# Grouped-query attention: value products in three fp32r products, two units behind the scores; rope sums and output parts on GpSimd

## The chip, the cores and the metric

One core of a Trainium2 chip runs the whole program in one launch. The metric is the device time of that launch in microseconds (us). The kernel before takes 2538.56 us, the median of three runs (2532.92 to 2539.3). Within 0.3% two kernels can't be told apart here.

## The reference

Two layers work on 1024 tokens (two batches of 512) of width 512. Each layer is attention and a feed-forward part, and after each of the four the result is added to its input and normalised. The change touches only the attention of the second layer, grouped-query attention with 32 query heads and 8 key/value heads of width 128:

```python
q = (hidden_states @ Wq).reshape(B, S, nh, hd).transpose(0, 2, 1, 3)
k = (hidden_states @ Wk).reshape(B, S, nkv, hd).transpose(0, 2, 1, 3)
v = (hidden_states @ Wv).reshape(B, S, nkv, hd).transpose(0, 2, 1, 3)
q = _apply_rope(q, cos, sin)        # x * cos + rotate_half(x) * sin
k = _apply_rope(k, cos, sin)
...                                 # k, v repeated for the 4 heads of a group
logits = jnp.einsum('bhqd,bhkd->bhqk', q, k) * scale      # then the causal mask
attn = jax.nn.softmax(logits.astype(jnp.float32), axis=-1).astype(q.dtype)
out = jnp.einsum('bhqk,bhkd->bhqd', attn, v)
return out.transpose(0, 2, 1, 3).reshape(B, S, nh * hd) @ Wo
```

## The kernel before

The stages run one after the other. In the stage of the change (`gqa_stage`) five engines run programs of their own, each in the order in which it is written, and wait for each other by counting semaphores. Each program is a loop over the eight key heads (`body`). The last body stands apart, since it has no next head to prepare.

A body has eight units (`NU`), one for each pair of a query head of the group (four) and a batch half (two). Unit `u` belongs to head `u // 2` and batch `u % 2`. Nearly every product is made in three: a number is split into a high part (rounded to fp32r) and a low part (the rest), and high x high, low x high and high x low are added up in PSUM (`TERMS`). Making the parts is a copy and a subtraction.

For a unit, TensorE first makes the scores of four row tiles (L1570 to L1583). A row tile `t` has (t + 1) * 128 columns, for the causal mask; together they take three banks (`ps_s`). VectorE takes the row maxima (L1484), ScalarE the exponentials with their row sums (L1423), VectorE the reciprocals (L1489) and the scaling of the rows in place (`normalise`, four instructions at L1493, SBUF to SBUF). TensorE transposes the rows in three pieces of 4, 4 and 2 tiles into two banks `ps_t` (L1593), pieces 1 and 3 of a unit in the same bank; ScalarE copies each piece to SBUF (L1430). TensorE multiplies it with the values in fp32 (`outputs`, L1603); this product alone is not made in three. ScalarE takes the high part of the result (L1436) and VectorE the low part (L1499).

The query of a unit is projected by 12 matmuls (L1558) two units ahead. Its rope is on VectorE: two multiplications by the sine into `by_sin` with the halves swapped (L1473, L1474), one by the cosine into `roped` (L1475), and the sum (L1477). GpSimd then makes the high part (L1357) and the low part (L1359) of the sum. GpSimd also splits the weights of this and the next head (L1337, L1339), one slice (two instructions) behind each rope. SP's queue loads the next weights once the old ones are split.

In a unit's turn `u`, TensorE's order is: scores of `u`, pieces 1 and 2 of `u - 1`, projection of the query of `u + 2`, piece 3 of `u - 1`, outputs of `u - 1`. VectorE's order is: maxima of `u`, normalise of `u`, rope of `u + 2`, low part of the outputs of `u - 1`. In turns 6 and 7 the next body's keys and queries are projected, in place of a query of this one (two projections and two ropes in each turn). After the eight turns each body multiplies the outputs of its four heads by their rows of `Wo` (`merge`, eight token tiles of 12 matmuls, L1614), and VectorE adds the result to `X` (L1520). At the start of a body, between the scores of unit 0 and unit 1, the values are projected, copied (L1410), transposed (L1567) and copied to `v1` (L1414).

## Time and profile before

| | us |
|---|---|
| median of three runs | 2538.56 |
| the profiled execution | 2530.54 |
| its span | 2528.8 |
| attention of the second layer, 1640 to 2465 | 825 |

| engine, whole span | busy us |
|---|---|
| TensorE, matmul | 2460.4 |
| TensorE, weight load | 1857.2 |
| VectorE | 1557.3 |
| ScalarE | 1393.4 |
| GpSimd | 1136.3 |

In the rows below PE is TensorE's matmul, PEld its weight load, DVE VectorE, ACT ScalarE and POOL GpSimd. L1593 is line 1593 of the kernel before. The durations of matmuls run into each other, since they are pipelined: what one costs is the distance from its start to the next start, its pitch.

### The profile page before, as it was taken

The page shows a single profiled execution, that of the slowest core. Times are in us where ns is not written, and L with a number is a line of the kernel's source. Part 1 is how long each engine was busy: PE and PEld are TensorE (multiplying, and loading weights), DVE is VectorE, ACT ScalarE, POOL GpSimd, SP SyncE. Part 2 cuts the span into 40 slices and gives each one's busy share as a digit, 9 for nine tenths or more (in the row PEclk, how much of TensorE's full clock was granted, in tenths as well). Part 3 has the DMA queues.
Part 4 walks back from the last instruction along what each step waited for, and adds up shares of the span by engine and source line. Part 5 has one row for each costly group of instructions (what it writes and reads, how often), then busy time and mean ns, then how long its engine had stood idle before and what let it go on. Part 6 is the DMA issues. An engine that isn't in the chain of part 4 may idle for free. (4 is left out here: it accounts for less than half of the span.)

```text
span 2528.8 us, 40532 instructions
## 1 busy us (share of the span) xinstructions
PE 2460.4 (97%) x12630; PEld 1857.2 (73%) x12630; DVE 1557.3 (62%) x2790; ACT 1393.4 (55%) x2155; POOL 1136.3 (45%) x1140
## 2 busy tenths in 40 slices
PE   8999999999999999999998999899999999999997
PEld 4777777777777777777775688687787887878774
DVE  7666666666666666666664523474755756557556
ACT  4777777777777777777776423242423424324231
POOL 1555555565656555555554334143424335234210
PEclk9999999999999999999999999999999999999998
DMA  6222222222222222222223222101001000010001
GB/s 214 45 53 44 53 47 58 45 53 44 53 47 53 45 53 53 44 53 44 55 49 88 96 88 88 71 26 42 17 25 41 16 26 18 23 41 17 1 1 55
DMA packets 47611, 125.39 MB, mean 50 GB/s; under 512 B 6033, under 2 KB 23441, under 8 KB 41426
## 3 DMA queue, kind: packets, MB, share of 16 engines
q1 hardware_dynamic: 47570, 124.85, 18.4%
q8 instruction: 25, 0.41, 0.1%
q14 instruction: 16, 0.13, 0.0%
HBM read 80.27 MB, written 10.49 MB: 36 GB/s over the span
## 5 line engine op out<-in xcount | busy, mean ns | idle before, releaser
L427 DVE TENSOR_REDUCE row_max<-ps_max 128x1 f32<-128x512 f32 x1024 | 670.8, 688 | 187.6 <-PE ps_max L517 165.5
L292 POOL TENSOR_TENSOR p_parts<-probs,p_parts 128x1024 f16<-128x1024 f32 x256 | 547.6, 2149 | 360.1 <-ACT p_parts L346 359.1
L341 ACT ACTIVATE probs<-ps_score 128x1024 f32<-128x1024 f32 x512 | 523.4, 1023 | 238.9 <-PE ps_score L533 217.0
L531 PE MATMUL ps_score<-Q,K 128*128 128x512 f32 x1024 | 406.9, 397 | 2.7 <-ACT probs L341 2.2
L533 PE MATMUL ps_score<-Q,K 97*128 97x512 f32 x1024 | 406.3, 397 | 0.0
L517 PE MATMUL ps_max<-KX,Q 68*128 68x512 f32 x1024 | 377.9, 410 | 2.4 <-DVE row_max L427 2.3
L421 DVE TENSOR_TENSOR Q<-ps_x,Q 64x512 fp32r<-64x512 f32 x254 | 175.1, 689 | 241.1 <-ACT Q L336 237.4
L346 ACT ACTIVATE p_parts<-probs 128x1024 f16<-128x1024 f32 x256 | 269.5, 1053 | 4.1
L517 PEld LDWEIGHTS ps_max<-KX,Q 68*128 68x128 f32 x1024 | 189.1, 189 | 74.4 <-issue 27.3
L531 PEld LDWEIGHTS ps_score<-Q,K 128*128 128x128 f32 x1024 | 194.0, 189 | 60.7 <-ACT probs L341 9.6
L1357 POOL CAST q_hi<-roped 128x512 fp32r<-128x512 f32 x64 | 39.2, 612 | 416.5 <-DVE roped L1477 198.4
L533 PEld LDWEIGHTS ps_score<-Q,K 97*128 97x128 f32 x1024 | 194.7, 190 | 39.7
L1423 ACT ACTIVATE probs<-ps_s,minus_max 128x512 f32<-128x512 f32 (+3 forms) x256 | 131.8, 541 | 138.5 <-DVE minus_max L1484 138.5
L1430 ACT ACTIVATE probsT<-ps_t 128x512 f32<-128x512 f32 (+1 forms) x192 | 94.1, 525 | 176.2 <-PE ps_t L1593 175.8
L336 ACT ACTIVATE Q<-ps_x 64x512 fp32r<-64x512 f32 x254 | 150.7, 593 | 72.5 <-PE ps_x L502 71.0
L1603 PE MATMUL ps_o<-probsT,v 128*128 128x512 f32 (+3 forms) x512 | 149.2, 434 | 1.3 <-ACT probsT L1430 1.3
L502 PE MATMUL ps_x<-xl,w_hi 128*128 128x512 f32 x508 | 143.6, 405 | 0.0
L502 PE MATMUL ps_x<-xh,w_hi 128*128 128x512 f32 x508 | 139.2, 396 | 0.0
L502 PE MATMUL ps_x<-xh,w_lo 128*128 128x512 f32 x508 | 138.4, 395 | 0.0
L1436 ACT ACTIVATE o_hi<-ps_o 128x512 fp32r<-128x512 f32 x64 | 38.4, 599 | 168.0 <-PE ps_o L1603 168.0
L544 PE MATMUL ps_o<-probs,V_slot 128*32 128x512 f32 x1024 | 123.1, 598 | 3.4 <-ACT probs L341 3.4
L1520 DVE TENSOR_TENSOR X<-ps_r,X 128x512 f32<-128x512 f32 x64 | 44.3, 692 | 132.9 <-PE ps_r L1614 132.9
(269 smaller groups left out, 4418.6 us busy)
## 6 DMA issues: line engine op xcount, KB each, us to landing
Q<-Q SPq DMA_DIRECT2D x64, 512.0 KB, 4.3
ffn_raw<-in_w_ffn SPq DMA_DIRECT2D x22, 768.0 KB, 4.3
w_raw<-in_w_qrope SPq DMA_DIRECT2D x32, 512.0 KB, 3.6
wq_raw<-in_wq SPq DMA_DIRECT2D x8, 1024.0 KB, 5.5
wo_raw<-in_wo SPq DMA_DIRECT2D x8, 1024.0 KB, 4.9
content_k<-probs SPq DMA_DIRECT2D x8, 512.0 KB, 6.4
Q<-content_q SPq DMA_DIRECT2D x64, 64.0 KB
K<-content_k SPq DMA_DIRECT2D x64, 64.0 KB
```

The source lines that it names most:

```text
L292: pool.tensor_tensor(p_lo[:, j, :, :], probs[:, j, 0:PAIRED, :], p_hi[:, j, :, :], ALU.subtract)\
L336: ins = act.activation(Q2[0:ROPE, b, 2 * pair + k, :], src[k * ROPE:(k + 1) * ROPE, :], ACT.Copy)
L341: act.activation(probs[:, j, 2 * half:2 * half + 2, :], ps_score[half][:, :, :], ACT.Exp, scale=SCALE).then_inc(exped, 1)
L346: act.activation(p_hi[:, j, :, :], probs[:, j, 0:PAIRED, :], ACT.Copy).then_inc(p_high, 1)
L421: ins = dve.tensor_tensor(Q1[ROPE:P, b, 2 * pair + k, :], src[k * ROPE:(k + 1) * ROPE, :], Q2[0:ROPE, b, 2 * pair + k, :], ALU.subtract)
L427: dve.tensor_reduce(row_max[:, t, j:j + 1], ps_max[t % 2][:, :], axis=AXX, op=ALU.max)\
L502: last = pe.matmul(out[:, :], w[:, c, pair, :], sb[x][:, c, b * S:(b + 1) * S], start=third == c == 0, stop=third == 2 and c == DC - 1)
L517: pe.matmul(ps_max[t % 2][:, :], Q2[0:KC0, b, j, t * P:(t + 1) * P], KX[0:KC0, b, j, :], start=True, stop=True).then_inc(max_made, 1)
L531: pe.matmul(ps_score[half][:, k, :], K1[:, b, t * P:(t + 1) * P], Q1[:, b, j, :], start=True, stop=False)
L533: last = pe.matmul(ps_score[half][:, k, :], K2[0:MROW + 1, b, j, t * P:(t + 1) * P], Q2[0:MROW + 1, b, j, :], start=False, stop=True)
L1423: act.activation(probs[:, u % 2, t, 0:n], ps_s[bank][:, at:at + n], ACT.Exp, bias=minus_max[:, t:t + 1], accum_out=sums[:, u % 2, t:t + 1] ...
L1603: last = pe.matmul(ps_o[:, tile * P:S], V[:, b, tile, :], probsT[:, k, at:at + S - tile * P], start=tile == 0, stop=k == 2)
```

## The change

- Value products are made in three, as the others: `V` and `probsT` get a high and a low part. ScalarE copies the high parts; VectorE makes the low parts, of the values (`low_values`) and of the three pieces of each unit (`low_turned`). A bank `ps_t` is free once the low part is made. `outputs` has 12 matmuls where it had 4 in fp32.
- The outputs of a unit and piece 3 of its transposes go one turn later: TensorE's order in turn `u` is scores of `u`, piece 3 of `u - 2`, projection, outputs of `u - 2`, pieces 1 and 2 of `u - 1`.
- VectorE's order in turn `u` is: maxima of `u`, low part of piece 3 of `u - 2`, rope of `u + 2` without its sum, normalise of `u`, low parts of pieces 1 and 2 of `u - 1`.
- The rope's sum moves to GpSimd, in front of its high and low part. `by_sin` has two buffers.
- ScalarE copies the outputs unsplit to `o_raw` (two buffers), and GpSimd makes both parts (`split_out`), behind the rope of the unit four later.
- The rows of a unit are packed in `probs` one behind the other (1280 numbers) in place of four rows of 512.
- The merges begin with the heads that are ready: they go head by head, with waits for the last two. Piece 3 of unit 7 and its outputs stand between the merges.

```diff
-        V = buf("v1", [P, NB, ST, P])
-        by_sin = buf("by_sin", [P, S])
+        V = [buf(f"v_{k}", [P, NB, ST, P], F32R) for k in ("hi", "lo")]
+        by_sin = buf("by_sin", [P, 2, S])
         roped = buf("roped", [P, 2, S])
-        probs = buf("probs1", [P, 2, ST, S])
-        probsT = buf("probsT", [P, 3, S])
+        ROWS = [P * t * (t + 1) // 2 for t in range(ST + 1)]
+        probs = buf("probs1", [P, 2, ROWS[ST]])
+        TURNED = [(0, S), (S, S), (2 * S, 2 * P)]
+        probsT = [buf(f"probsT_{k}", [P, 2 * S + 2 * P], F32R) for k in ("hi", "lo")]
+        values_T = probs[:, 1, 0:NB * S].rearrange("p (b s) -> p b s", b=NB)
+        o_raw = buf("o_raw", [P, 2, S])
...
-            def rope(n, at, parts):
-
+            def rope(n, at, parts, take):
+
+                pool.wait_ge(taken, take + 1)
+                pool.sem_inc(gate_pool, 1)
+                pool.tensor_tensor(roped[:, at, :], roped[:, at, :], by_sin[:, at, :], ALU.add).then_inc(summed, 1)
                 pool.wait_ge(summed, n + 1)
                 pool.sem_inc(gate_pool, 1)
                 pool.tensor_copy(parts[0], roped[:, at, :]).then_inc(r_high, 1)
                 pool.wait_ge(r_high, n + 1)
+                pool.sem_inc(gate_pool, 1)
                 pool.tensor_tensor(parts[1], roped[:, at, :], parts[0], ALU.subtract).then_inc(r_low, 1)
...
+            def split_out(i, u):
+
+                pool.wait_ge(o_taken, ONE + i + 1)
+                pool.sem_inc(gate_pool, 1)
+                pool.tensor_copy(O[0][:, u % 2, u // 2, :], o_raw[:, u % 2, :]).then_inc(o_step, 1)
+                pool.wait_ge(o_step, i + 1)
+                pool.sem_inc(gate_pool, 1)
+                pool.tensor_tensor(O[1][:, u % 2, u // 2, :], o_raw[:, u % 2, :], O[0][:, u % 2, u // 2, :],
+                                   ALU.subtract).then_inc(o_low, 1)
...
-                    rope_query(r + u - 2, u, u % 2)
+                    rope_query(r + u - 2, u, u % 2, tk + take_query(u))
+                    if u >= 4:
+                        split_out(i + u - 4, u - 4)
...
-                        rope_key(r + NU - 2 + 2 * b, b)
-                        rope_query(r + NU - 1 + 2 * b, b, 1)
+                        rope_key(r + NU - 2 + 2 * b, b, tk + take_next(2 * b))
+                        if b == 1:
+                            split_out(i + NU - 3, NU - 3)
+                            split_out(i + NU - 2, NU - 2)
+                        rope_query(r + NU - 1 + 2 * b, b, 1, tk + take_next(2 * b + 1))
                         if b == 0:
+                            split_out(i + NU - 4, NU - 4)
                             split_kv(1, s + n + 1)
+                    split_out(i + NU - 1, NU - 1)
                     for h in range(1, GQ):
                         split_q(h, s + n + 1 + h)
+                else:
+                    for u in range(NU - 4, NU):
+                        split_out(i + u, u)
 
...
+                act.wait_ge(o_low, i + 1)
+                act.activation(o_raw[:, u % 2, :], ps_o[:, :], ACT.Copy).then_inc(o_taken, 1)
...
+                softmax(i, 0, ALL)
                 values(kv, 0)
                 values(kv, 1)
                 turned_values(kv, 0)
                 turned_values(kv, 1)
                 for u in range(1, NU):
+                    if u >= 2:
+                        act.wait_ge(turned, 3 * (i + u - 1))
+                    softmax(i + u, u, BEGIN)
+                    if u >= 2:
+                        take_turned(kv, u - 2, 2)
+                    softmax(i + u, u, REST)
+                    if u >= 2:
+                        take_outputs(kv, u - 2)
                     take_turned(kv, u - 1, 0)
                     take_turned(kv, u - 1, 1)
-                    softmax(i + u, u)
-                    take_turned(kv, u - 1, 2)
-                    take_outputs(kv, u - 1)
+                take_turned(kv, NU - 2, 2)
+                take_outputs(kv, NU - 2)
...
-                dve.tensor_tensor(by_sin[0:h, :], ps[h:P, :], tables[0:h, sin, :], ALU.mult)
-                dve.tensor_tensor(by_sin[h:P, :], ps[0:h, :], tables[h:P, sin, :], ALU.mult)
+                dve.tensor_tensor(by_sin[0:h, at, :], ps[h:P, :], tables[0:h, sin, :], ALU.mult)
+                dve.tensor_tensor(by_sin[h:P, at, :], ps[0:h, :], tables[h:P, sin, :], ALU.mult)
                 dve.tensor_tensor(roped[:, at, :], ps[:, :], cos, ALU.mult).then_inc(taken, 1)
-                dve.wait_ge(taken, take + 1)
-                dve.tensor_tensor(roped[:, at, :], roped[:, at, :], by_sin[:, :], ALU.add).then_inc(summed, 1)
...
+            def low_values(kv, b):
+                dve.wait_ge(v_high, NB * kv + b + 1)
+                dve.tensor_tensor(V[1][:, b, :, :], ps_t[b][:, :].rearrange("p (t n) -> p t n", t=ST), V[0][:, b, :, :],
+                                  ALU.subtract).then_inc(v_low, 1)
+
+            def low_turned(i, u, k):
+                dve.wait_ge(t_high, 3 * i + k + 1)
+                at, n = TURNED[k]
+                dve.tensor_tensor(probsT[1][:, at:at + n], ps_t[(u + k) % 2][:, 0:n], probsT[0][:, at:at + n],
+                                  ALU.subtract).then_inc(t_low, 1)
...
+                for b in range(NB):
+                    low_values(kv, b)
                 rope(r, ring + ring_query(2), (START + ring_query(2)) % 2, 0, tk, 0)
+
+                def rope_next(at):
+                    rope(r + NU - 2 + at, ring + ring_next(at), (START + ring_next(at)) % 2, 1 - at % 2,
+                         tk + take_next(at), at % 2)
+
                 for u in range(1, NU):
                     maxima(i + u)
-                    normalise(i + u, u)
+                    if u >= 2:
+                        low_turned(i + u - 2, u - 2, 2)
                     if u < NU - 2:
                         rope(r + u, ring + ring_query(u + 2), (START + ring_query(u + 2)) % 2, 0, tk + u, u % 2)
-                        low_o(i + u - 1, u - 1)
-                    else:
-                        for k in range(2) if not last else ():
-                            at = 2 * (u % 2) + k
-                            rope(r + NU - 2 + at, ring + ring_next(at), (START + ring_next(at)) % 2, 1 - k, tk + take_next(at), k)
-                        low_o(i + u - 1, u - 1)
+                    elif not last:
+                        for at in (0, 1) if u == NU - 2 else (2,):
+                            rope_next(at)
+                    normalise(i + u, u)
+                    low_turned(i + u - 1, u - 1, 0)
+                    low_turned(i + u - 1, u - 1, 1)
+                low_turned(i + NU - 2, NU - 2, 2)
+                if not last:
+                    rope_next(3)
+                low_turned(i + NU - 1, NU - 1, 0)
+                low_turned(i + NU - 1, NU - 1, 1)
                 add_out(0)
-                add_out(1)
-                low_o(i + NU - 1, NU - 1)
-                for j in range(2, TT):
+                low_turned(i + NU - 1, NU - 1, 2)
+                for j in range(1, TT):
...
-                pe.wait_ge(o_low, ONE + i)
-                for k, piece in enumerate(pieces):
-                    pe.wait_ge(t_taken, 3 * i + k + 1)
-                    for tile, at in piece:
-                        last = pe.matmul(ps_o[:, tile * P:S], V[:, b, tile, :], probsT[:, k, at:at + S - tile * P],
-                                         start=tile == 0, stop=k == 2)
+                pe.wait_ge(o_taken, ONE + i)
+                for p, vs in ((0, (0, 1)), (1, (0,))):
+                    for k, piece in enumerate(pieces):
+                        pe.wait_ge((t_high, t_low)[p], (0, TWO)[p] + 3 * i + k + 1)
+                        for v in vs:
+                            for tile, at in piece:
+                                at += TURNED[k][0]
+                                last = pe.matmul(ps_o[:, tile * P:S], V[v][:, b, tile, :],
+                                                 probsT[p][:, at:at + S - tile * P],
+                                                 start=tile == p == v == 0, stop=k == 2 and p == 1)
                 last.then_inc(pv_made, 1)
...
-            def merge(last, tk, j):
+            def merge(last, tk, i, j):
 
                 at = ring_out(last, j)
                 pe.wait_ge(taken, tk + take_out(last, j) - 1)
                 k = 0
-                for o, w in TERMS:
-                    for h in range(GQ):
+                for h in range(GQ):
+                    if j % ST == 0 and h >= GQ - 2:
+                        pe.wait_ge(o_low, TWO + i + 2 * h + j // ST + 1)
+                    for o, w in TERMS:
...
                     scores(i + u, u, r + u - 2)
-                    if u == 1:
-                        pe.wait_ge(v_ready, NB * (kv + 1))
-                    turn(i + u - 1, u - 1, 0)
-                    turn(i + u - 1, u - 1, 1)
+                    if u >= 2:
+                        turn(i + u - 2, u - 2, 2)
                     if u < NU - 2:
                         query(u + 2)
                     elif not last:
-                        b = u % 2
-                        pe.wait_ge(wkv_split, 2 * kv + 3)
-                        pe.wait_ge(taken, tk + take_next(2 * b) - 1)
-                        project(wkv, 0, b, (START + ring_next(2 * b)) % 2)
-                        pe.wait_ge(wq_split, GQ * (kv + 1) + 1)
-                        pe.wait_ge(taken, tk + take_next(2 * b + 1) - 1)
-                        project(wq, 0, b, (START + ring_next(2 * b + 1)) % 2)
-                    turn(i + u - 1, u - 1, 2)
-                    outputs(i + u - 1, u - 1)
-                for k in range(3):
-                    turn(i + NU - 1, NU - 1, k)
+                        key_next(u % 2)
+                        if u == NU - 2:
+                            query_next(0)
+                    if u >= 2:
+                        outputs(i + u - 2, u - 2)
+                    if u == 1:
+                        pe.wait_ge(v_low, NB * (kv + 1))
+                    turn(i + u - 1, u - 1, 0)
+                    turn(i + u - 1, u - 1, 1)
+                turn(i + NU - 2, NU - 2, 2)
+                if not last:
+                    query_next(1)
+                outputs(i + NU - 2, NU - 2)
+                turn(i + NU - 1, NU - 1, 0)
+                turn(i + NU - 1, NU - 1, 1)
                 pe.wait_ge(wo_split, GQ * (kv + 1))
-                pe.wait_ge(o_low, ONE + i + NU - 1)
-                merge(last, tk, 0)
-                merge(last, tk, 1)
+                merge(last, tk, i, 0)
+                turn(i + NU - 1, NU - 1, 2)
+                merge(last, tk, i, 1)
+                merge(last, tk, i, 2)
                 outputs(i + NU - 1, NU - 1)
-                merge(last, tk, 2)
-                merge(last, tk, 3)
-                pe.wait_ge(o_low, ONE + i + NU)
-                for j in range(ST, TT):
-                    merge(last, tk, j)
+                for j in range(3, TT):
```

## Rows read from the trace of the kernel before

**Rows 1.** Windows: window, its length, busy time and instructions of each engine, clock granted, DMA.
```profile
1640.00:2465.00 825.00, 809.46 (x4156) 662.20 (x4154) 508.92 (x1032) 288.08 (x806) 292.83 (x312) 1.00 0.06 22
```

**Rows 2.** Waits of TensorE, 1640 to 2465: who for whom, total, times, longest.
```profile
PE ps_r L1614 <- DVE o_lo L1499: 9.0, 7, 1.3
```

**Rows 3.** Timeline of TensorE, one turn: start, duration, engine, line, operation.
```profile
1904.17 1.06 PE L1593 MATMUL ps_t<-ident,probs 128*128 128x128 f32 x8
1904.98 1.18 PE L1558 MATMUL ps_r<-xh,wq_hi 128*128 128x512 f32 x4
...
1908.05 2.32 PE L1603 MATMUL ps_o<-probsT,v 128*128 128x512 f32 x8
1910.02 0.58 PE L1580 MATMUL ps_s<-k_hi,q_hi 128*128 128x512 f32 x1
1910.44 0.40 PE L1580 MATMUL ps_s<-k_hi,q_lo 128*128 128x512 f32 x1
1910.67 0.39 PE L1580 MATMUL ps_s<-k_lo,q_hi 128*128 128x512 f32 x1
...
1911.37 0.34 PE L1580 MATMUL ps_s<-k_lo,q_hi 128*128 128x384 f32 x1
1911.55 0.22 PE L1581 MATMUL ps_s<-mask_sb 128*128 128x128 f32 x1
1911.61 0.27 PE L1580 MATMUL ps_s<-k_hi,q_hi 128*128 128x128 f32 x1
...
1912.52 1.05 PE L1593 MATMUL ps_t<-ident,probs 128*128 128x128 f32 x8
```

**Rows 4.** Timeline of the same turn, VectorE and GpSimd.
```profile
1901.16 0.69 DVE L1473 TENSOR_TENSOR by_sin<-ps_r,tables 64x512 f32<-64x512 f32 x1
...
1903.29 0.69 DVE L1477 TENSOR_TENSOR roped<-roped,by_sin 128x512 f32<-128x512 f32 x1
...
1903.90 0.68 DVE L1499 TENSOR_TENSOR o_lo<-ps_o,o_hi 128x512 fp32r<-128x512 f32 x1
...
1904.14 0.61 POOL L1357 CAST q_hi<-roped 128x512 fp32r<-128x512 f32 x1 [4.43 <-DVE roped L1477]
...
1904.50 1.68 DVE L1484 TENSOR_REDUCE minus_max<-ps_s 128x1 f32<-128x512 f32 x4
...
1907.98 0.18 DVE L1489 RECIPROCAL inverse<-sums 128x4 f32<-128x4 f32 x1 [1.80 <-ACT probs L1423]
...
1908.19 1.28 DVE L1493 TENSOR_SCALAR probs<-probs,inverse 128x128 f32<-128x128 f32 x4
```

**Rows 5.** First body's normalise beside GpSimd, then L1493 from 1662 on (ns min/median/max).
```profile
1656.56 1.30 POOL L1339 TENSOR_TENSOR wq_lo<-wq_raw,wq_hi 128x512 fp32r<-128x512 f32 x1
1656.80 3.61 DVE L1493 TENSOR_SCALAR probs<-probs,inverse 128x128 f32<-128x128 f32 x4
1657.80 0.61 POOL L1337 CAST wq_hi<-wq_raw 128x512 fp32r<-128x512 f32 x1
1658.49 1.29 POOL L1339 TENSOR_TENSOR wq_lo<-wq_raw,wq_hi 128x512 fp32r<-128x512 f32 x1
...
L1493 DVE TENSOR_SCALAR probs<-probs,inverse x252: 285/382/489, 1668.1 to 2436.9; 128x128 f32<-128x128 f32 x63, 128x384 f32<-128x384 f32 x63
```

**Rows 6.** Timeline at the start of a body, all engines.
```profile
1967.38 1.07 PE L1558 MATMUL ps_r<-xh,wq_hi 128*128 128x512 f32 x4
...
1970.51 0.69 DVE L1473 TENSOR_TENSOR by_sin<-ps_r,tables 64x512 f32<-64x512 f32 x1 [4.09 <-PE ps_r L1558]
...
1970.77 1.09 ACT L1414 ACTIVATE v<-ps_t 128x512 f32<-128x512 f32 x2 [2.59 <-PE ps_t L1567]
1970.92 0.48 PE L1580 MATMUL ps_s<-k_hi,q_hi 128*128 128x512 f32 x1
```

**Rows 7.** Timeline of TensorE: the first score matmul of two bodies in a row.
```profile
1857.03 0.39 PE L1580 MATMUL ps_s<-k_hi,q_hi 128*128 128x512 f32 x1
...
1959.54 0.39 PE L1580 MATMUL ps_s<-k_hi,q_hi 128*128 128x512 f32 x1
```

More of the change, by code:

```diff
@@ L1358, in rope, with rope_key, rope_query @@
                 pool.wait_ge(r_high, n + 1)
+                pool.sem_inc(gate_pool, 1)
                 pool.tensor_tensor(parts[1], roped[:, at, :], parts[0], ALU.subtract).then_inc(r_low, 1)
-            def rope_key(n, b):
-                rope(n, 0, [k[:, b, :] for k in K])
-            def rope_query(n, u, at):
-                rope(n, at, [q[:, u % 2, :] for q in Q])
+            def rope_key(n, b, take):
+                rope(n, 0, [k[:, b, :] for k in K], take)
+            def rope_query(n, u, at, take):
+                rope(n, at, [q[:, u % 2, :] for q in Q], take)
+            def split_out(i, u):
[6 more added lines that the diff above has]
+                                   ALU.subtract).then_inc(o_low, 1)
+            pool.sem_inc(o_low, TWO)
             for b in range(NB):
-                rope_key(2 * b, b)
-                rope_query(2 * b + 1, b, 1)
+                rope_key(2 * b, b, 2 * b)
+                rope_query(2 * b + 1, b, 1, 2 * b + 1)
             pool.wait_ge(wq_split, 2)
@@ L1376, in body @@
                 s = FIRST + GQ - 2 + EACH * kv
+                tk = START + TAKEN * kv
+                i = NU * kv
                 n = 0
@@ L1409, in values, with softmax @@
                 act.wait_ge(made, START + PER * kv + b + 1)
-                act.activation(probsT[:, b, :], ps_r[(START + b) % 2][:, :], ACT.Copy).then_inc(v_taken, 1)
+                act.activation(values_T[:, b, :], ps_r[(START + b) % 2][:, :], ACT.Copy).then_inc(v_taken, 1)
             def turned_values(kv, b):
                 act.wait_ge(v_turned, NB * kv + b + 1)
-                act.activation(V[:, b, :, :], ps_t[b][:, :].rearrange("p (t n) -> p t n", t=ST), ACT.Copy)\
-                   .then_inc(v_ready, 1)
-            def softmax(i, u):
-                for k, t in enumerate((3, 2, 0, 1)):
+                act.activation(V[0][:, b, :, :], ps_t[b][:, :].rearrange("p (t n) -> p t n", t=ST), ACT.Copy)\
+                   .then_inc(v_high, 1)
+            def softmax(i, u, part):
+                for k, t in list(enumerate((3, 2, 0, 1)))[part]:
                     act.wait_ge(maxed, ST * i + (3 if k == 1 else k + 1))
@@ L1422, in softmax @@
                     n = (t + 1) * P
-                    act.activation(probs[:, u % 2, t, 0:n], ps_s[bank][:, at:at + n], ACT.Exp,
+                    act.activation(probs[:, u % 2, ROWS[t]:ROWS[t] + n], ps_s[bank][:, at:at + n], ACT.Exp,
                                    bias=minus_max[:, t:t + 1], accum_out=sums[:, u % 2, t:t + 1]).then_inc(exped, 1)
@@ L1465, in rope @@
                 dve.wait_ge(made, ring + 1)
-                if not first:
-                    dve.wait_ge(summed, n)
                 if not first and not second:
@@ L1566, in turn_values @@
                 for t in range(ST):
-                    last = pe.transpose(ps_t[b][:, t * P:(t + 1) * P], probsT[:, b, t * P:(t + 1) * P], ident[:, :])
+                    last = pe.transpose(ps_t[b][:, t * P:(t + 1) * P], values_T[:, b, t * P:(t + 1) * P], ident[:, :])
                 last.then_inc(v_turned, 1)
```

43 lines of the change are left out of this document (25 added, 18 removed).

## The prediction, made before the changed kernel ran

> **What bounds the kernel now.** I read the windows first: the changed stage is 825 of 2528.8 us and TensorE is busy in 809.5 of them, VectorE in 509, ScalarE in 288 and GpSimd in 293, with TensorE's clock granted in full (the 2.4 GHz level) [rows 1]. The waits of TensorE in it are small; the largest is 1.3 us, once for each key head but the last [rows 2]. So before the change TensorE's order of work is the length of the stage. The timeline of one inner unit (one head of one batch half; 64 of them, eight in each of eight bodies) repeats every 8.35 us (1904.17 to 1912.52) [rows 3]. What decides this prediction are VectorE and GpSimd, which have room in the sum, and the question whether they have it at the same moments.
>
> **Value products (TensorE).** The fp32 products of a unit are eight records from 1908.05 to 1910.02, and the first score matmul behind them takes 0.42 to the next (1910.44), where an fp32r matmul of 512 columns has a pitch of 0.23 (1910.44 to 1910.67): 1.97 and 0.19 of change-over, 2.16 us [rows 3]. New are three products of four matmuls: 512 columns at 0.23, 384 at 0.18 (1911.37 to 1911.55), 128 at 0.06 behind a long one (1911.55 to 1911.61), 256 between these two, I take 0.12, and some 0.05 lost behind each short one: 1.9 us. Bounds: 1.77 (nothing lost behind the short ones) and 2.1 (each 128 and 256 a tenth dearer than I take them). Scores now follow fp32 transposes; what that change-over costs I bound by 0 and the 0.19 just read, and take 0.1. Gain: 0.16 us for a unit, 1.3 for a body, 10 in all, if TensorE remains the bound (-0.1 to 0.39 a unit, -6 to 25 in all).
>
> **Other work moved.** VectorE loses the rope sum (0.69, 80 times) and the low part of the outputs (pitch 0.60, 64 times) and gains three low parts of the transposed rows per unit (0.60, 0.60 and some 0.35, by the 0.60 pitch and half the columns): about +0.3 us a unit [rows 4]. Two low parts of the values are added per body (0.69 each). ScalarE does the same number of copies, in another order; it is 35% busy, so this costs nothing unless it delays what it feeds. GpSimd gains a rope sum, which it never ran here: bounds 0.61 (its cast, one input) and 2.6 (twice its subtraction), and I take the subtraction's own 1.30, which has the same shape and two inputs [rows 5]; what it is longer or shorter goes straight into the loop below. It gains an output split too (0.69 + 1.24 by start-to-start [rows 5]). Its step is then 1.37 + 0.69 + 1.24 for the rope, 1.93 for the outputs and 1.93 for a weight split: 7.2 us in a unit of 8.2. It fits, and the weight loads behind it on SP's queue move some 13 us later in a body, where they have over 30 us. Packed rows and the second by_sin buffer change addresses only: no term.
>
> **Where the wait appears.** In the new order VectorE runs: maxima, low part 3 of the unit before last, three rope multiplications, normalise, low parts 1 and 2. TensorE's transposes of piece 3 (in front of the next query projection) wait for low part 1, because they write the same bank; the projection feeds the rope; the rope stands in front of the normalise on VectorE; and that in front of low part 1. This is a loop, with length
> 0.2 (release, by the 0.16 from VectorE's end at 1903.98 to GpSimd's start at 1904.14 [rows 4]) + 0.2 (two transposes at 0.10, eight in 0.81 [rows 3]) + 0.1 + 3.13 (projection's first matmul to the rope's first instruction, 1967.38 to 1970.51 [rows 6]) + 2.13 (three multiplications, 1901.16 to 1903.29 [rows 4]) + N + 0.69 (low part 1) = 6.45 + N.
> N runs from the rope's last multiplication to the end of the normalise. In before it is 1.5 (reciprocal at 1907.98, its scalings to 1909.47 [rows 4]). Then the loop is 7.95 us and hides under TensorE's 8.2.
>
> **What N becomes.** Four scalings take 1.28 us together in rows 4, where GpSimd is idle. One of the 64 normalises met a busy GpSimd: its four took 3.61 us (1656.80 to 1660.41) while GpSimd ran 1656.56 to 1657.86, 1657.80 to 1658.41 and 1658.49 to 1659.78 at its usual durations; the other 252 scalings were never above 489 ns [rows 5]. Three scalings, each behind one whole GpSimd instruction, explain it: the fourth, with GpSimd done, was quick. VectorE instructions that read PSUM show nothing of this: the maxima at 1904.50 take their 1.68 beside GpSimd's split from 1904.14 [rows 4]. In before the normalise stands ahead of the rope and GpSimd idles 4.4 us until the rope is summed [rows 4]. The change puts it right behind the rope's last multiplication, and this is also what starts GpSimd's sum: 0.17 later, the first scaling 0.24 later. So each scaling meets one of: sum, cast, subtraction, and the cast of the next split. The fourth ends 0.17 + 1.37 + 0.69 + 1.24 + 0.61 + 0.37 = 4.45 after the rope, or 4.1 if it slips in ahead of the next cast; I take N = 4.3. Bounds: 1.5 (as before) and 4.45. The loop is 10.75 us against 8.2, and TensorE stands still for the rest: its cheaper products lie inside this wait and return nothing.
>
> A rule of the Trainium skill speaks against this change: "SBUF — State Buffer", section "SBUF: two separate sides", says that VectorE in a mode with two ports and GpSimd exclude each other for a whole instruction rather than share. With that rule, the trace agrees in the one place it can (3.61 against 1.28). Were bandwidth shared instead, N would be nearer 2.8, which is the second rival.
>
> **The sum for a body**, from its first score matmul. The values' second copy ends at 1971.86 and scores of unit 1 start 11.38 after the body's [rows 6]; behind it low parts of values to 13.1, rope of unit 2 to 15.3, GpSimd's sum, cast and subtraction to 18.8. Scores of unit 2 would be due at 17.4 (11.38 + 2.38 + 2.75 + 0.9): they wait 1.6 us. Maxima of unit 1 to 16.9, rope of unit 3 to 19.05, normalise with GpSimd busy (weights, then its sum) to 23, first piece-3 transposes at 23.9. Then four loops of 10.75 (66.9), one of 10.75 + 2.75 with the next key projection (80.4), one of 10.75 (91.2), last query projection, outputs, eight transposes (5.9, to 97.1), and eight merges of 12 x 0.228 with one piece 3 and one outputs (24.0): 121.1 us. Before it is 102.5 (1857.03 to 1959.54 [rows 7]). Seven bodies: 7 x 18.6 = 130. The last has no next projections; units 1 to 5 lose 2.5 + 4 x 2.4, and some 1.5 where nothing fills a wait: 14. Start of the stage: scores of unit 0 wait for GpSimd's two longer ropes, 1. Together +145 us on the profiled execution's 2530.5 (span 2528.8 and 1.7 around it): 2676. The median of the runs shown is 8 us above that execution; I forecast 2680 between both.
>
> **Rivals.**
> 1. *The scalings are not held up* (N stays under 1.7). For it: one single case in before carries the argument; against it: three scalings in a row were stretched there, and the collision is triggered by the same event in each unit. Then per body: -1.3 products, +1.6 at the start, +0.4 at the end (piece 3 of unit 6 waits 2.0 in place of 0.3 + 1.3), +0.7 in all, with 1 and 2 at the ends of the stage +8: 2546 by the median.
> 2. *Half held up*: only one or two scalings wait, N near 2.8, loop 9.25; seven loops less 1.5 in eight bodies is 80 less: 2600.
> 3. *Faster*: as 1, and the three products cost their 1.77 with no change-over, 0.39 a unit or 3.1 a body, against 2.0 lost at start and end: -1.1 a body, 2530. It decides from N under 1.7 and more than 0.25 us gained per unit; against it that fp32r matmuls of 128 columns show a pitch that their columns don't explain.
> 4. *GpSimd late with the output parts*: merge 0 needs unit 6's, 2.8 us after its products; it has 2.9. If late by one split, +1.9 a body: 2695, inside my range.
>
> **Chances.** Forecast with 4: 0.72 (2640 to 2720). Rival 2: 0.09. Rival 1: 0.10, most of it within the 0.3% (7.6 us) that a measurement of this kernel can't tell from no change. Rival 3: 0.09. Slower 0.72 + 0.09 + 0.03 = 0.84, same 0.07, faster 0.09. Range 2575 to 2725: it takes in N from 2.8 up and leaves out rivals 1 and 3.
>
> **What would show it.** Scalings of the normalise with means of 0.9 us and more where they were 0.30 to 0.48, the stage near 970 us, TensorE's largest wait on VectorE's low part of the transposed rows some 2.5 us per unit, and busy shares of TensorE in the stage falling from 98% to near 83%. Product group at 1.9 us by start-to-start. Wrong if the scalings keep their 0.30 to 0.48 with GpSimd busy, or if scores, not piece 3, are what waits.

## The result and the profile after

The changed kernel takes 2613.57 us (median of 4 runs, 2607.76 to 2617.49) against 2538.93 (4 runs, 2532.92 to 2542.43): slower by the ratio 1.0294, interval 1.0272 to 1.0315. The forecast was 2680 with a range of 2575 to 2725. The sign came as forecast, and scalings held up by GpSimd are the cause, as forecast; the size is about half. The band of 2640 to 2720, which had 0.72, is missed. The time lies in the range only because the range reaches down to rival 2 (2600), which had 0.09.

The windows of the changed stage, of one body with the clock granted in full and of the last body. The columns are those of [rows 1]: length, then busy time and instructions of PE, PEld, DVE, ACT and POOL, the granted clock, the DMA share and GB/s.

```profile
1640.00:2546.00 906.00, 823.62 (x4444) 707.46 (x4442) 620.57 (x1113) 291.00 (x819) 528.13 (x524) 0.98 0.06 23
2109.00:2218.95 109.95, 100.50 (x554) 86.72 (x552) 75.54 (x136) 35.70 (x101) 66.76 (x66) 1.00 0.07 23
2443.60:2546.00 102.40, 91.63 (x505) 78.64 (x503) 72.06 (x133) 34.19 (x100) 43.04 (x42) 0.98 0.00 1
```

Against [rows 1] this window is 81 us longer, and TensorE is busy in 91% of it where it was 98%. Of the 81 us, 11 lie ahead of the stage: its first projection starts at 1648.73, in before at 1637.57. A body at the full clock takes 109.95 us where it took 102.5 [rows 7]. VectorE is busy 112 us more (620.6 against 508.9). Some 20 of them are work: the low parts that it gained are 119 us (81.7 + 27.2 + 10.3), the rope sums and output parts that it lost 99 (55.4 + 43.8). Another 88 are the scalings, which are as many as before and are held up. By form, the four scalings of the normalise in the stage (busy time, mean ns of one | idle ahead):

```profile
L1534 DVE TENSOR_SCALAR probs<-probs,inverse 128x256 f32<-128x256 f32 x64 | 70.4, 1100 | 0.0
L1534 DVE TENSOR_SCALAR probs<-probs,inverse 128x512 f32<-128x512 f32 x64 | 56.2, 879 | 0.0
L1534 DVE TENSOR_SCALAR probs<-probs,inverse 128x384 f32<-128x384 f32 x64 | 35.9, 560 | 0.0
L1534 DVE TENSOR_SCALAR probs<-probs,inverse 128x128 f32<-128x128 f32 x64 | 25.9, 404 | 2.2
```

In before these forms took 354, 482, 433 and 300 ns, 100.5 us together; now it is 188.4. The 256 columns take three times their time, the 512 not quite twice; the 384 and the 128 take some 0.1 us more. These means mix units of different kinds, which are told apart below. The waits of the stage (us in total, times, longest):

```profile
POOL roped L1364 <- DVE roped L1517: 212.0, 51, 20.2
PE ps_t L1650 <- DVE probsT_lo L1545: 61.8, 56, 2.8
PE ps_s L1638 <- POOL q_lo L1370: 13.3, 9, 1.5
```

TensorE's large wait is the one forecast, the transposes of piece 3 for VectorE's low part 1, 56 times, but at 1.1 us a time, not 2.5 (0.57 in the units of the loop). The first row says that GpSimd's sum waits for the end of VectorE's rope, 51 times for 80 sums, so the two are in step in most units. Two groups of GpSimd show a thing that the sum had left out (stage up to 2460; the last figure is the idle time ahead):

```profile
L1346 POOL TENSOR_TENSOR wq_lo<-wq_raw,wq_hi 128x512 fp32r<-128x512 f32 x30 | 38.8, 1294 | 2.4
L1370 POOL TENSOR_TENSOR q_lo<-roped,q_hi 128x512 fp32r<-128x512 f32 x58 | 74.1, 1278 | 10.4 <-POOL q_hi L1367 10.4
```

Both subtractions wait for the cast ahead of them. The first, which the change leaves alone, starts 0.08 us (2.4 / 30) behind it. The second, where the change puts one more signal (`pool.sem_inc(gate_pool, 1)`) between the two, starts 0.18 us (10.4 / 58) behind. The same signal stands between the sum and the cast of the rope. So the change, besides moving work to GpSimd, opens gaps of 0.17 to 0.18 us in it.

One unit in the timeline (start, duration, engine; in brackets the idle ahead and what ended it). VectorE, with the four scalings one by one:

```profile
1931.73 0.69 DVE L1517 TENSOR_TENSOR roped<-ps_r,tables 128x512 f32<-128x512 f32 x1
1932.55 0.29 DVE L1534 TENSOR_SCALAR probs<-probs,inverse 128x128 f32<-128x128 f32 x1
1932.75 1.38 DVE L1534 TENSOR_SCALAR probs<-probs,inverse 128x256 f32<-128x256 f32 x1
1934.05 0.41 DVE L1534 TENSOR_SCALAR probs<-probs,inverse 128x384 f32<-128x384 f32 x1
1934.39 0.83 DVE L1534 TENSOR_SCALAR probs<-probs,inverse 128x512 f32<-128x512 f32 x1
1935.13 1.27 DVE L1545 TENSOR_TENSOR probsT_lo<-ps_t,probsT_hi 128x512 fp32r<-128x512 f32 x2
```

GpSimd at the same time:

```profile
1932.61 1.37 POOL L1364 TENSOR_TENSOR roped<-roped,by_sin 128x512 f32<-128x512 f32 x1 [1.13 <-DVE roped L1517]
1934.15 0.79 POOL L1367 CAST q_hi<-roped 128x512 fp32r<-128x512 f32 x1 [0.17 <-POOL roped L1364]
1935.11 1.27 POOL L1370 TENSOR_TENSOR q_lo<-roped,q_hi 128x512 fp32r<-128x512 f32 x1 [0.18 <-POOL q_hi L1367]
```

TensorE:

```profile
1927.00 0.44 PE L1650 MATMUL ps_t<-ident,probs 128*128 128x128 f32 x2 [0.56 <-DVE probsT_lo L1545]
1930.04 0.39 PE L1663 MATMUL ps_o<-probsT_hi,v_hi 128*128 128x512 f32 x1
1931.96 1.04 PE L1650 MATMUL ps_t<-ident,probs 128*128 128x128 f32 x8
1932.75 0.48 PE L1638 MATMUL ps_s<-k_hi,q_hi 128*128 128x512 f32 x1
1933.07 0.40 PE L1638 MATMUL ps_s<-k_hi,q_lo 128*128 128x512 f32 x1
1935.87 0.44 PE L1650 MATMUL ps_t<-ident,probs 128*128 128x128 f32 x2 [0.57 <-DVE probsT_lo L1545]
```

The loop is read from the two PE rows with brackets: 1927.00 to 1935.87, 8.87 us, with a wait of 0.57 in it. Before, TensorE's own order had 8.35 for such a unit [rows 3]. The normalise, from the end of the rope to the last scaling, runs from 1932.42 to 1935.22: N = 2.8 us, where the forecast had 4.3. The first scaling starts 0.06 us ahead of GpSimd's sum and escapes (0.29 us). The second (256 columns) is held up: it ends 0.15 us behind the sum's end at 1933.98, after 1.38 us. The third (384) starts in GpSimd's gap of 0.17, 0.10 ahead of the cast, and takes 0.41. The fourth (512) is held up until the cast ends at 1934.94, and ends 0.11 us behind the start of GpSimd's subtraction. Two of four are held up.

In the six inner bodies units 2 to 5 and unit 7 look like this one (2.6 to 2.7 us for the four). In unit 0 GpSimd is idle and the four take 1.28. In unit 1 they meet a weight split and then the sum (3.5), in unit 6 the end of a key's low part and then the sum (3.3).

### The profile page after: what moved, and what is told of

The parts are those of the page before. It is cut to its first block and busy times, and to the rows that moved or that the text cites. A ratio compares the mean times of both kernels' runs of the same rounds, so it can differ in the third digit from the quotient of the medians.

```text
span 2610.2 us, 41954 instructions
## 1 busy us (share of the span) xinstructions
PE 2477.5 (95%) x12886; PEld 1898.4 (73%) x12886; DVE 1659.3 (64%) x2854; ACT 1388.5 (53%) x2155; POOL 1369.5 (52%) x1348
## 5 line engine op out<-in xcount | busy, mean ns | idle before, releaser
L1364 POOL TENSOR_TENSOR roped<-roped,by_sin 128x512 f32<-128x512 f32 x80 | 107.1, 1339 | 222.7 <-DVE roped L1517 212.0
L1534 DVE TENSOR_SCALAR probs<-probs,inverse 128x128 f32<-128x128 f32 (+3 forms) x256 | 173.0, 736 | 2.2
L1650 PE MATMUL ps_t<-ident,probs 128*128 128x128 f32 x640 | 94.3, 278 | 61.8 <-DVE probsT_lo L1545 61.8
L1471 ACT ACTIVATE o_raw<-ps_o 128x512 f32<-128x512 f32 x64 | 38.3, 599 | 190.9 <-PE ps_o L1663 190.9
```

The source lines that it names most:

```text
L1534: ins = dve.tensor_scalar(row, row, inverse[:, t:t + 1], None, ALU.mult)
```

## The experiments

Medians, and ratios to the kernel before on the same chip with their intervals. The kernel before has medians of 2535.86 to 2540.11 on these chips, so differences of a few us between two rows are to be read from the ratios:

| kernel | what differs | us | ratio |
|---|---|---|---|
| after | | 2613.57 | 1.0294 (1.0272 to 1.0315) |
| e2_late | first scaling 0.1 later | 2612.57 | 1.0317 (1.0285 to 1.0350) |
| e8_sum_waits | rope sum behind the normalise | 2571.76 | 1.0154 (1.0131 to 1.0176) |
| e1_scale_act | scalings on ScalarE | 2529.39 | 0.9977 (0.9963 to 0.9991) |
| e3_sum_dve | rope sum on VectorE | 2690.54 | 1.0623 (1.0599 to 1.0647) |
| e4_no_out | no output split | 2603.68 | 1.0258 (1.0237 to 1.0278) |
| e11_wide | wider gap on GpSimd | 2586.88 | 1.0198 (1.0175 to 1.0221) |
| e7_both | e1 + rope of unit 2 earlier | 2520.39 | 0.9926 (0.9910 to 0.9943) |
| e12_best | e7 + last query projection earlier | 2507.41 | 0.9874 (0.9857 to 0.9891) |
| e13_fp32_values | e12 with fp32 value products | 2520.77 | 0.9937 (0.9921 to 0.9952) |

**Who starts first (e2_late).** A second reciprocal, whose result nobody reads, puts VectorE's first scaling behind the start of GpSimd's sum. It takes 0.18 us but overlaps its neighbours, so that the scaling starts 0.1 us later (0.91 us behind the start of the rope's last multiplication, in the changed kernel 0.82).

```
+        unused = buf("unused", [P, ST])
...
+                dve.reciprocal(unused[:, :], sums[:, u % 2, :])
```

> The changed kernel with a second, unused reciprocal (0.17 us) between the reciprocal and the four scalings on VectorE. Theory (a scaling and a GpSimd instruction exclude each other; who starts first wins): in the changed kernel the first scaling starts 0.06 us ahead of GpSimd's rope sum and escapes; 0.17 later it loses. Then the first scaling takes 1.2 us or more (0.40 mean in the changed kernel), N (rope's end to normalise's end) grows from 2.8 to between 3.0 and 4.2, and the time to 2650 us (2625 to 2690). Rival (the two only share bandwidth, or GpSimd's load matters and not the order): nothing but the added 0.17 us in some 50 loops, 9 us: 2622, and the first scaling stays near 0.40.

2612.57 us; by the ratios 0.0023 above the changed kernel, some 6 us, with intervals that overlap. Two of the scalings by form, and the timeline:

```profile
L1536 DVE TENSOR_SCALAR probs<-probs,inverse 128x128 f32<-128x128 f32 x64 | 64.8, 1012 | 0.0
L1536 DVE TENSOR_SCALAR probs<-probs,inverse 128x256 f32<-128x256 f32 x64 | 30.0, 468 | 0.0
```

```profile
1938.37 1.29 POOL L1365 TENSOR_TENSOR roped<-roped,by_sin 128x512 f32<-128x512 f32 x1 [1.17 <-DVE roped L1518]
1938.41 2.68 DVE L1536 TENSOR_SCALAR probs<-probs,inverse 128x128 f32<-128x128 f32 x4
1938.41 1.34 DVE L1536 TENSOR_SCALAR probs<-probs,inverse 128x128 f32<-128x128 f32 x1
1939.83 0.65 POOL L1368 CAST q_hi<-roped 128x512 fp32r<-128x512 f32 x1 [0.17 <-POOL roped L1365]
1940.66 1.55 POOL L1371 TENSOR_TENSOR q_lo<-roped,q_hi 128x512 fp32r<-128x512 f32 x1 [0.18 <-POOL q_hi L1368]
```

The scaling of 128 columns now starts 0.04 us behind the sum in place of 0.06 ahead of it, and takes 1.34 us in this unit in place of 0.29 (means 1012 and 404 ns). The 256 falls from 1100 to 468: it has taken the place in the gap. This is all or nothing by the order of starts, and slower sharing of one bandwidth would not do it: the same scaling overlaps the same sum in both kernels. The expectation of the time was wrong all the same. It let every scaling behind the first wait in full; instead the rest shifted among the gaps, and the four stayed at 2.68, which is what they take in the changed kernel too. The loop is longer by the later start alone (8.96 us, from 1932.78 to 1941.74 in its trace, against 8.87). The rival's time, 9 us above the changed kernel, is not refuted: some 6 us were measured, with an interval that holds both 0 and 9. It is the durations that decide, and they refute its other sign, a first scaling near 0.40.

**Taking the collision away, from GpSimd's side (e8_sum_waits).** GpSimd waits for the normalise before it sums the rope.

```
+                    pool.wait_ge(normed, i + u - 1)
...
+                        pool.wait_ge(normed, i + NU - 1 + b)
```

> The changed kernel, GpSimd waits with the rope's sum until the normalise behind that rope is done. GpSimd's own chain gets 1.3 us longer. Theory (collision): scalings fall back near 0.30 to 0.48 us except where GpSimd's last weight split still runs; N 1.5 to 2.3, the loop under TensorE's 8.2; 2555 us (2540 to 2580). Rival (the delay is GpSimd's long chain or the new order itself): not faster, 2613 or up to 2640.

2571.76: it gives back about half of the loss (42 of the 75 us by the medians, 0.0140 of 0.0294 by the ratios) and lies 17 us above what was expected. The collision is not gone. In 24 of the 64 normalises the four take 1.3 us; in the others they still meet a weight split or another GpSimd instruction and take 1.9 to 4.0. The difference is seen in two normalises of this kernel, one with GpSimd idle and one in a unit where a weight split is still running:

```profile
1933.02 1.27 DVE L1536 TENSOR_SCALAR probs<-probs,inverse 128x128 f32<-128x128 f32 x4
...
1921.70 2.36 DVE L1536 TENSOR_SCALAR probs<-probs,inverse 128x128 f32<-128x128 f32 x4
...
1922.04 1.41 POOL L1346 TENSOR_TENSOR wo_lo<-wo_raw,wo_hi 128x512 fp32r<-128x512 f32 x1
```

With GpSimd idle the four take the 1.27 that they took in before [rows 4].

**From VectorE's side (e1_scale_act).** The scalings go to ScalarE, behind its copies of pieces 1 and 2; VectorE keeps the reciprocal, and `inverse` gets two buffers. Everything else of the change stays.

```
+            def scale(i, u):
+                act.wait_ge(inverted, i + 1)
+                for t in range(ST):
+                    row = probs[:, u % 2, ROWS[t]:ROWS[t + 1]]
+                    ins = act.activation(row, row, ACT.Copy, scale=inverse[:, u % 2, t:t + 1])
+                ins.then_inc(normed, 1)
...
-                for t in range(ST):
-                    n = (t + 1) * P
-                    row = probs[:, u % 2, ROWS[t]:ROWS[t + 1]]
-                    ins = dve.tensor_scalar(row, row, inverse[:, t:t + 1], None, ALU.mult)
-                ins.then_inc(normed, 1)
```

> The changed kernel with the four scalings on ScalarE, behind the copies of pieces 1 and 2; VectorE keeps only the reciprocal. Theory: no VectorE instruction is left that GpSimd holds up, low part 1 is ready early, TensorE is the bound at 8.2 us a unit but for 1.5 us at the start of each body: 2545 us (2530 to 2565), no dips of the clock in the stage's later part. Rival (the schedule two units behind, or GpSimd being 80% busy, costs the time): 2600 or more.

2529.39, ratio 0.9977: the whole loss is gone, and a little more. This run takes the four scalings themselves off VectorE too, 1.28 us in a unit even where nothing holds them up, so that it doesn't separate their work from the collision; e8, e11 and the durations do that. ScalarE's scalings run beside GpSimd, and neither is longer for it (1.91 us in the 7 normalises with GpSimd idle, 1.91 to 1.96 in the others):

```profile
1906.14 1.93 ACT L1477 ACTIVATE probs<-probs,inverse 128x128 f32<-128x128 f32 x4
1906.59 0.61 POOL L1367 CAST q_hi<-roped 128x512 fp32r<-128x512 f32 x1 [0.17 <-POOL roped L1364]
1907.38 1.28 POOL L1370 TENSOR_TENSOR q_lo<-roped,q_hi 128x512 fp32r<-128x512 f32 x1 [0.18 <-POOL q_hi L1367]
```

TensorE's wait for the low part falls from 61.8 us to 8.2, once a body, and the wait of unit 2's scores, 1.5 a time, stays:

```profile
PE ps_t L1655 <- DVE probsT_lo L1549: 8.2, 8, 1.1
```

**Undoing the move of the rope sum (e3_sum_dve).** The sum returns to VectorE.

```
-                pool.wait_ge(taken, take + 1)
-                pool.sem_inc(gate_pool, 1)
-                pool.tensor_tensor(roped[:, at, :], roped[:, at, :], by_sin[:, at, :], ALU.add).then_inc(summed, 1)
...
+                dve.wait_ge(taken, take + 1)
+                dve.tensor_tensor(roped[:, at, :], roped[:, at, :], by_sin[:, at, :], ALU.add).then_inc(summed, 1)
```

> The changed kernel with the rope's sum back on VectorE; all else, GpSimd's output split too, as changed. Theory: the scalings still collide, now with the high part's cast and the low part's subtraction, N stays near 2.8 while the rope on VectorE is 0.7 longer: loop 9.6, 2650 us (2625 to 2670). Rival (GpSimd has too much to do, and the sum is what broke it): faster than the changed kernel, 2560 to 2600.

2690.54: worse, as expected, and by 40 us more. In the new order the sum lies in the loop, and its 0.61 from start to start is not all. GpSimd then starts with its cast, and other scalings are caught: the first waits for the cast (0.72 us), the 384 for the subtraction, and it is caught most:

```profile
L1533 DVE TENSOR_SCALAR probs<-probs,inverse 128x384 f32<-128x384 f32 x64 | 83.0, 1297 | 0.0
```

```profile
1941.20 3.10 DVE L1533 TENSOR_SCALAR probs<-probs,inverse 128x128 f32<-128x128 f32 x4
1941.20 0.72 DVE L1533 TENSOR_SCALAR probs<-probs,inverse 128x128 f32<-128x128 f32 x1
1941.23 0.61 POOL L1364 CAST q_hi<-roped 128x512 fp32r<-128x512 f32 x1 [3.84 <-DVE roped L1516]
1942.02 1.30 POOL L1367 TENSOR_TENSOR q_lo<-roped,q_hi 128x512 fp32r<-128x512 f32 x1 [0.18 <-POOL q_hi L1364]
```

The first scaling waits although its recorded start is 0.03 us ahead of the cast's. So the recorded starts tell who was first only to some hundredths: at 0.03 ahead a scaling waits here, at 0.06 and more ahead none waits in the traces, and at 0.04 to 0.05 both occur. N is 3.1 to 3.3 and the loop 10.0 (1934.94 to 1944.95 in its trace). Stretches with TensorE at the 1.2 GHz level are more frequent too, 22 in the bodies where the changed kernel has 8. So in this order the sum on GpSimd helps. That the new place of the normalise is what hurts is argued from the collisions; no run puts it back in front of the rope.

**A wider gap on GpSimd (e11_wide).** Five signals in place of one between sum and cast.

```
-                pool.sem_inc(gate_pool, 1)
+                for _ in range(5):
+                    pool.sem_inc(gate_pool, 1)
```

> The changed kernel with four more semaphore increments on GpSimd between the rope's sum and the high part's cast. They do no work; they widen the gap between the two instructions, 0.17 us in the changed kernel. Theory: scalings get in only in such gaps; with some 0.4 us all three that the sum holds up get in before the cast, N falls from 2.8 to 2.4, and the kernel gets faster though GpSimd does more: 2590 us (2575 to 2605), mean of the 512-column scaling from 0.88 to 0.5. Rival (the gap plays no part): 2613 or a little more.

2586.88: slowing GpSimd makes the kernel 27 us faster (24 by the ratios). The last scaling finds the gap and falls from 879 to 625 ns, the others stay (1141, 562, 411); TensorE's wait goes with it. The scaling, and the waits of TensorE and of GpSimd's cast (0.49 us each, 31.5 / 64, where the changed kernel has 0.17):

```profile
L1535 DVE TENSOR_SCALAR probs<-probs,inverse 128x512 f32<-128x512 f32 x64 | 40.0, 625 | 0.0
```

```profile
PE ps_t L1651 <- DVE probsT_lo L1546: 42.1, 51, 2.5
POOL q_hi L1368 <- POOL roped L1364: 31.5, 64, 0.8
```

Closing the gap, the opposite, was not run, but the traces hold cases of a narrow one. In before's only collision [rows 5] the 384 starts 0.01 us ahead of the subtraction at 1658.49, behind a gap of 0.08, and waits for all of it. In unit 1 of the changed kernel's inner bodies the gap between a weight's cast and its subtraction is 0.08 as well. There the short first scaling had waited for the cast, the 256 starts 0.08 ahead of the subtraction and gets in. So what counts is how far ahead of GpSimd's next instruction the next scaling starts; a wider gap gives it more. Before, and two lines of the changed kernel:

```profile
1658.48 1.52 DVE L1493 TENSOR_SCALAR probs<-probs,inverse 128x384 f32<-128x384 f32 x1
1903.93 0.34 DVE L1534 TENSOR_SCALAR probs<-probs,inverse 128x256 f32<-128x256 f32 x1
1904.01 1.40 POOL L1346 TENSOR_TENSOR wo_lo<-wo_raw,wo_hi 128x512 fp32r<-128x512 f32 x1
```

**Is it GpSimd's load or its moment (e4_no_out)?** The output split is left out (1.9 us of GpSimd a unit): ScalarE writes the high part at once and the output projection uses it for the low part too, so that its matmuls stay as many. The low part of the outputs is missing from its result.

```
-                act.activation(o_raw[:, u % 2, :], ps_o[:, :], ACT.Copy).then_inc(o_taken, 1)
+                act.activation(O[0][:, u % 2, u // 2, :], ps_o[:, :], ACT.Copy).then_inc(o_taken, 1)
...
-                                        O[o][:, j // ST, h, (j % ST) * P:(j % ST + 1) * P], wo[w][:, h, :],
+                                        O[0][:, j // ST, h, (j % ST) * P:(j % ST + 1) * P], wo[w][:, h, :],
```

> The changed kernel without the output split: ScalarE writes the outputs' high part directly, GpSimd passes the semaphore on, and the low part isn't made (the merges use the high part twice; the low part of the outputs is left out of the result). GpSimd has 15 us less in each body of 110. Theory: in the steady loop the scalings meet only the three instructions of the rope, so N and the time don't change: 2610 us (2595 to 2620). Rival (GpSimd's total load sets the time): 2540 to 2590.

2603.68. A quarter of GpSimd's load is worth 10 us, and its dearest scaling stands as it was (1100 ns in the changed kernel):

```profile
L1530 DVE TENSOR_SCALAR probs<-probs,inverse 128x256 f32<-128x256 f32 x64 | 70.1, 1096 | 0.0
```

For the loop the moment decides, not the load.

**The start and the end of a body (e7_both, e12_best).** On top of e1, e7 takes the rope of unit 2 ahead of the low parts of the values on VectorE:

```
+                rope(r, ring + ring_query(2), (START + ring_query(2)) % 2, 0, tk, 0)
...
-                rope(r, ring + ring_query(2), (START + ring_query(2)) % 2, 0, tk, 0)
```

> Scalings on ScalarE (2529 us), and at the start of a body the rope of unit 2 in front of the low parts of the values on VectorE. Theory: takes away TensorE's wait of 1.5 us for the low part of query 2, once a body: 2518 us (2510 to 2525).

2520.39. On top of that, e12 has TensorE project the last query ahead of the piece-3 transposes of unit 6:

```
-                turn(i + NU - 2, NU - 2, 2)
...
+                turn(i + NU - 2, NU - 2, 2)
```

> As the one before, and TensorE projects the last query ahead of piece 3 of unit 6, which waits 1.1 us in each body for low part 1. Theory: 7 us less than the one before: 2511 us (2502 to 2520), against 2536 for the kernel before the change.

2507.41, ratio 0.9874 to before: faster than both kernels. Both waits of TensorE that e1 had left in each body are down to one case each in the stage (1.3 and 1.1 us), and TensorE is busy in 99% of it:

```profile
1650.00:2450.00 800.00, 793.85 (x4416) 692.01 (x4416) 447.92 (x844) 400.46 (x1065) 514.19 (x521) 1.00 0.06 23
```

**What the three products are worth where TensorE is the bound (e13_fp32_values).** e12 with the value products back in fp32; the low parts of values and transposed rows are not computed.

```
-                for p, vs in ((0, (0, 1)), (1, (0,))):
+                for p, vs in ((0, (0,)),):
```

> The best kernel (scalings on ScalarE, both waits of TensorE taken away, 2507 us) with the value products back in fp32 and no low parts of values and transposed rows on VectorE. What the three fp32r products are worth where TensorE is the bound. Theory: 0.16 us for a unit, 10 us: 2517 us (2512 to 2525). Rival (the gain was the order of work alone, and three products cost what one in fp32 does): 2507.

2520.77, 13 us above e12 (16 by the ratios). The intervals (0.9921 to 0.9952 and 0.9857 to 0.9891) don't touch. The change's first part does pay, 0.2 us a unit over 64 units, once the wait is gone that the change brought.

## Why the prediction was right in direction and too high

**Right: the loop and its wait.** The chain rope, normalise, low part 1, piece 3, projection decides the units, and TensorE waits at the place named. Its terms but N were 6.45 and are 6.07 (8.87 less 2.8): the release behind low part 1 takes 0.1 rather than 0.2, the 0.1 between the transposes and the projection is not there, low part 1 takes 0.6 from start to start, and the rest is some hundredths tighter. Value products are 1.92 from start to start (1930.04 to 1931.96), forecast 1.9, and the change-over to the scores is 0.1 (1932.75 to 1933.07, 0.32, less a pitch of 0.23), the value taken. Both lie in the wait, as said, and e12 against e13 shows what they are worth outside it.

**Right: the cause.** Held-up scalings beside a busy GpSimd. e1 removes the pair and the loss goes entirely; e8 keeps GpSimd's rope out of the normalise and about half goes; e11 slows GpSimd, lets one more scaling in, and 24 to 27 us go; e4 takes away GpSimd work that is not at that moment, and 10 us go. That scalings wait for whole instructions, which rested on one normalise in [rows 5], e2 shows by 404 against 1012 ns for a shift of 0.1 us in the starts. The signs named came out smaller, though: one form's mean in four is above 0.9 us (1.10), the window is 906 us and not 970, the wait 1.1 and not 2.5, TensorE's busy share 91% and not 83%.

**Wrong in size: N, 4.3 taken and 2.8 measured.** This is the step that failed. The prediction had "each scaling meets one of: sum, cast, subtraction, and the cast of the next split". It assumed that GpSimd's sum starts first, 0.17 against 0.24 behind the rope, a margin of 0.07 us worked out from starts in other surroundings. In fact the sum starts 0.19 behind it and the scaling 0.13. And it took GpSimd's gaps as they are in before, 0.08 at most, though the diff shows a signal more in each of them. The gaps are 0.17: the scaling behind the one that waited goes in there, and the next one then waits for the instruction behind the gap. The collision in [rows 5] that served as the model had the narrow gaps. So two scalings wait, not four: rival 2's count, which got 0.09 for want of a reason. The loops are shorter than forecast, 1.9 us in each of four (1.5 by N and 0.4 by the other terms), 1.2 in the fifth and 1.9 in the sixth, 10.6 us of a body; another 0.6 comes from the first piece 3, at 23.3 us of the body and not 23.9. A body is longer by 7.44 and not by 18.6.

In the Trainium skill, "SBUF — State Buffer", section "SBUF: two separate sides", a VectorE instruction in a mode with two ports and a GpSimd instruction exclude each other, and whichever starts first has the shared ports for its whole instruction. With that rule e2's 404 and 1012 ns agree (0.29 and 1.34 us in one unit). The prediction had set N near 2.8 both for shared bandwidth and for one or two scalings that wait. The measured 2.8 is the second: single scalings wait in full and others not at all, which the time by itself could not tell and the durations could.

**Right: unit 2's scores.** Forecast wait 1.6, measured 1.50, followed by the first wait for a low part, 1.61:

```profile
2128.12 0.49 PE L1638 MATMUL ps_s<-k_hi,q_hi 128*128 128x512 f32 x1 [1.50 <-POOL q_lo L1370]
```

**The last body** is 7 us longer (102.40 against 95.4) where 14 was forecast, by the same N and one stretch of lower clock.

**Left out: the clock.** The forecast had TensorE at its full level throughout. In the changed kernel it falls to the 1.2 GHz level for a few us seven times in the first seven bodies and once in the last, against once in before. Each time it falls within 1.5 us of the end of a wait of 1.6 to 2.8 us. One of them:

```profile
2240.00:2246.00 6.00, 4.36 (x17) 3.47 (x17) 4.82 (x9) 2.42 (x9) 5.05 (x5) 0.72 0.00 0
```

```profile
2242.26 0.50 PE L1650 MATMUL ps_t<-ident,probs 128*128 128x128 f32 x2 [1.64 <-DVE probsT_lo L1545]
2242.45 2.03 PE L1616 MATMUL ps_r<-xh,wq_hi 128*128 128x512 f32 x4
```

Four projection matmuls take 2.03 in place of 1.18, behind an idle stretch of 1.64. A body with such a stretch is 1.6 us longer (1997.49 to 2109.00, 111.51, against 109.95).

**The difference of the two profiled spans**, 81.4 us, is then: seven bodies 52.1 (7 x 7.44) and 9.3 of lower clock, last body 7.0, start of the stage 1.4 (1 forecast), 0.4 behind the stage, and 11.2 ahead of it, in code that didn't change. There a stretch of 27.3 us at the 1.2 GHz level begins at 48 us, where the profile of before has 6.8 us at 47. The profiles of e1, e7 and e12 have 27.3 there too, those of e3, e8 and e11, which hold the moved work as well, 3.4 to 10 us. So it doesn't come with the change as such; what sets its length is open. The medians differ by 74.6 us, less than the two profiled executions. Of the 145 forecast, 78 too many in seven bodies and 7 in the last, and 9 + 11 not foreseen.

## What to carry to other kernels

Before moving a VectorE instruction that reads and writes SBUF, list what GpSimd runs at that moment, above all if the same event releases both; each such pair can cost a whole GpSimd instruction, and here ScalarE did the same work beside GpSimd at no such cost. How many are held up hangs on starts that differ by 0.1 us, which a trace of another order doesn't give: let the range hold every count, with a chance for each, rather than take all. And look at the moment, not at the load: a quarter less GpSimd work gained 10 us, and a GpSimd slowed on purpose 27.

## What the runs showed of the hardware that was not expected

- One more signal between two dependent GpSimd instructions widens the gap between them from 0.08 to 0.17 us, five to 0.49. At 0.17 the scaling behind the one that had waited goes in too; at 0.49 one more does (879 to 625 ns). At 0.08 it goes in behind a waiting scaling of 128 columns (0.34 us for the 256) and not behind one of 256 (1.52 us for the 384).
- The recorded starts tell who is first to some hundredths of a us: 0.06 ahead or more a scaling always went, 0.03 ahead it waited (0.72 us in e3).
- GpSimd pays as well: in e2 its subtraction took 1.55 in place of 1.28, its cast 0.65, and in the changed kernel the cast 0.79, in place of 0.61. Its sum took 1.37 behind the scaling that was first, and 1.29 in e2.
- TensorE at the 1.2 GHz level for a few us at a time, next to waits of 1.3 to 4 us in a stage where it is otherwise busy: once before, eight times after, 22 times in e3 with its longer waits (up to 4.0 us), none inside the bodies in the profiles of e1, e7 and e12, where the waits are mostly gone.
